# The causal mask of the scores as sixteen 32-row products instead of four 128-row ones

## The chip, the cores and the metric

The kernel runs on one core of one Trainium2 chip. The metric is the device time of one execution in microseconds, the median of several runs.

## The reference

A decoder layer over 32 sequences (batches) of 256 tokens with 512 features. It has three parts, each followed by an addition to its input and a layer norm:

1. causal self-attention with 16 heads of 32 features and rotary positions,
2. an mLSTM cross part with 4 heads over a context,
3. attention over 4 heads of 64 features, which a router picks from 16 for each sequence.

The change lies in the first part. Cut to what matters there:

```python
qkv = x @ Wqkv
q, k, v = jnp.split(qkv, 3, axis=-1)            # 16 heads of 32
q, k = _apply_rope(q, k)
dist = idx[None, :] - idx[:, None]              # key minus query
allowed = (dist <= 0) & (dist >= -(w - 1))      # w = 256 = the sequence: causal only
scores = jnp.einsum('bhqd,bhkd->bhqk', q, k) / jnp.sqrt(jnp.float32(d))
scores = jnp.where(allowed[None, None], scores, -jnp.inf)
weights = jax.nn.softmax(scores, axis=-1)
out = jnp.einsum('bhqk,bhkd->bhqd', weights, v)
```

## The kernel before

Three stages, `a` (self-attention), `b` (mLSTM) and `c` (routed attention), work at the same time on three successive batches. Every stage is a generator on each engine; `in_turns` walks one step of the pipeline, and the strings in `ORDER` say, engine by engine, which stage's generator comes next. So every engine's program is a fixed sequence written out by hand, the same in each of the 34 steps (30 of them have all three stages). What binds engines to each other is semaphores: `Port.wait_ge` puts a wait ahead of an instruction.

All products of TensorE (PE) go through the helper `mm` (L581), all transposes through `tr` (L589), so the profile tells them apart by their tiles. Projections are made of three products each in fp32r halves (`mm3`).

The 16 heads go in four groups of four, `u` = 0 to 3. `scores(u)` makes the scores of the four heads of a group: it waits for the rotated q and k (`roped`) and for the exponentials that free the score banks (`exped`), then issues for the first 128 queries four products of 32 rows of the array (head j sits in rows 32j to 32j+31 and writes bank `ps_s[:, j]`), then four for the last 128 queries over all 256 keys. After that come four products over the whole array that add the causal mask: for each head `eye_bf` (a 128x128 identity in bf16) times `mask_bf` (-1e30 above the diagonal), into the two diagonal 128x128 blocks of its bank. The last of them raises `scored`, for which VectorE (DVE) waits in `maxes` (L1219); ScalarE (ACT) then makes the exponentials (`exps`, L931).

The four groups of a batch stand at four places of a step. This text calls them by what TensorE's program has next behind the mask:

- **place A** (u = 0): the products `ps_g<-log_f,const` of stage b,
- **place B** (u = 1): the projection `ps_g<-x_t_hi,w_sel_hi` of stage c,
- **place C** (u = 2): the transposes `ps_g<-const,p_a` of this stage,
- **place D** (u = 3): the products `ps_g<-pt_all,v_f` of stage c.

Other names: `p_t` the transposed exponentials (copied out of PSUM by ACT L982 and DVE L1248), `k_f` stage c's keys (DVE L1441), `x_t_lo` the low half of a transposed operand (DVE L1472 for stage c's output), `v_a` the values of stage a (ACT L946).

Of the kernel before, what the change touches and what calls it, by code (L numbers as in the profile page):

```python
# [5 lines left out]
BF16 = mybir.dt.bfloat16  # L6
# [6 lines left out]
P = 128  # L13
NB, T, D = 32, 256, 512
TT, KT = T // P, D // P
HA, DA = 16, D // 16
# [3 lines left out]
DX = D // HX  # L20
# [4 lines left out]
Q_SCALE = float(np.float32(1.0 / np.sqrt(DA)))  # L25
LN_EPS, MLSTM_EPS, RMS_EPS = 1e-5, 1e-6, 1e-6
MASKED = -1e30
LOWEST = -3e38


# [75 lines left out]
    return np.concatenate([a.astype(np.float32) for a in parts.values()], axis=1), where  # L106


def build(nc, x, ctx, wqkv, wout, igk, igb, fgk, fgb, rms, wq, bq, wk, bk, wv, bv, wr, br, wo, bo, out):

    def sb(name, shape, dt=F32):
        return nc.alloc_sbuf_tensor(name, shape, dt).ap()
# [9 lines left out]
    const = sb("const", [P, table.shape[1]])  # L122
    c = {n: const[:, a:b] for n, (a, b) in where.items()}
    eye, upto = c["eye"], c["upto"]
    eye_bf = sb("eye_bf", [P, P], BF16)
    mask_bf = sb("mask_bf", [P, P], BF16)

    wqkv_s = halves("wqkv", [P, KT, 3 * D])
    wout_s = halves("wout", [P, KT, D])
# [4 lines left out]
    rms_w = sb("rms_w", [P, DX])  # L134
    bias_col = sb("bias_col", [P, 3, HF])
    wr_s = sb("wr_s", [P, KT, HF])
    br_s = sb("br_s", [1, HF])
    wo_s = halves("wo", [P, KF * DF // P, D])
    bo_s = sb("bo_s", [P, D])
# [13 lines left out]
    p_t = sb("p_t", [P, 4, CAUSAL])  # L153
# [54 lines left out]
    ps_s = nc.alloc_psum_tensor("ps_s", [P, 4, D], F32).ap()  # L208
# [3 lines left out]
    def count(name, per=1):  # L212
        return Count(nc, name, per)
# [3 lines left out]
    stage_hi, stage_split, tables_ready, half_ready = count("stage_hi"), count("stage_split"), count("tables_ready"), count("half_ready")  # L217
# [276 lines left out]
    def in_turns(s, engine, stages):  # L494
# [4 lines left out]
        for n, g in live.items():  # L499
# [5 lines left out]
    col = lambda w: w.rearrange("(k p) n -> p k n", p=P)  # L505
    row = lambda b, n: b.unsqueeze(0).to_broadcast([P, n])
# [6 lines left out]
    columns = [(wgate[:, :, j * HX:(j + 1) * HX], col(g[i * D:(i + 1) * D, :])) for i, wgate in enumerate((wgate_q, wgate_k, wgate_v)) for j, g in enumerate((igk, fgk))]  # L513
    columns += [(bias_col[half * DF:(half + 1) * DF, j, :], b.rearrange("(h d) -> d h", d=DF)) for j, b in enumerate((bq, bk, bv)) for half in range(2)]
    singles = [(const, nc.inline_tensor(table, name="tables").ap()), (gate_bias[:, 0:HX], row(igb, HX)), (gate_bias[:, HX:], row(fgb, HX)),
               (p_t[:, 0, 0:P], nc.inline_tensor(np.triu(np.full((P, P), MASKED, np.float32), 1), name="mask").ap()), (rms_w, row(rms, DX)), (wr_s, col(wr)), (br_s, br.unsqueeze(0)), (bo_s, row(bo, D))]
    SETUP = 16 * (len(columns) + len(singles))
    PIECES, Q_PIECES = len(pieces), 2

# [57 lines left out]
    def tensor(engine):  # L577
        pe = Port(engine)

        def mm(o, l, r, first, last):  # L580
            return nc.tensor.matmul(o, l, r, start=first, stop=last)  # L581
# [6 lines left out]
        def tr(o, i, ident):  # L588
            return nc.tensor.transpose(o, i, ident)  # L589
# [11 lines left out]
        def stage_a(b):  # L601
# [34 lines left out]
            def scores(u):  # L636
                pe.wait_ge(*roped(b, u + 1))
                if b or u:
                    pe.wait_ge(*(exped(b, 2 * u) if u else exped(b - 1)))
                for t in range(TT):  # L640
                    for j in range(4):
                        rows = slice(DA * j, DA * j + DA)
                        o = ps_s[:, j, t * P:t * P + P * (t + 1)]
                        done = mm(o, qk[rows, 2 * u, t * P:(t + 1) * P], qk[rows, 2 * u + 1, 0:P * (t + 1)], t == 0, False)
                for j in range(4):
                    o = ps_s[:, j, :].rearrange("p (a n) -> p a n", a=2)[:, :, 0:P]
                    done = mm(o, eye_bf, mask_bf.unsqueeze(1).to_broadcast([P, 2, P]), False, True)
                done.then_inc(scored.sem)

            yield from rotary(0)  # L650
            yield from values(0)
            scores(0)
            for _ in range(5):
                yield
            yield from values(1)
            yield from rotary(1)
            for u in range(QUADS):
                if u + 1 < QUADS:
                    scores(u + 1)
                for _ in range(3):  # L660
                    yield
                for p in (2 * u, 2 * u + 1):
                    for j in range(2):
                        o = bank[("turn", 2 * p + j), b]
                        pe.wait_ge(*exped(b, p + 1))
                        pe.wait_ge(*freed[("turn", 2 * p + j), b])
                        for n in range(3):
                            done = tr(o[:, n * P:(n + 1) * P], p_a[p % 2][:, j, n * P:(n + 1) * P], eye)
# [15 lines left out]
                o = bank[("att", u), b]  # L684
# [7 lines left out]
                for k in range(TT):  # L692
                    for j in range(4):
                        h = 4 * u + j
# [3 lines left out]
                        done = mm(o[strip, cols], v_a[:, k, h * DA:(h + 1) * DA], w, k == 0, k == TT - 1)  # L698
# [220 lines left out]
        pe.wait_ge(setup_loaded.sem, SETUP)  # L919
        pe.wait_ge(half_ready.sem, 5)  # L920
        pe.wait_ge(stage_split.sem, PIECES)
        pe.wait_ge(tables_ready.sem, 5)
        for s in range(NB + 2):
            in_turns(s, "tensor", {"a": stage_a, "b": stage_b, "c": stage_c})

# [1 line left out]
    def scalar(engine):  # L927
        act = Port(engine)
# [238 lines left out]
            else:  # L1167
                nc.scalar.copy(dst[0], stages[n % len(stages)]).then_inc(stage_hi.sem)
        act.wait_ge(setup_loaded.sem, SETUP)
        act.wait_ge(tables_ready.sem, 5)  # L1170
        act.wait_ge(half_ready.sem, 5)
        act.wait_ge(stage_split.sem, PIECES)
        for s in range(NB + 2):
# [3 lines left out]
    def vector(engine):  # L1177
        dve = Port(engine)
        v = nc.vector
# [112 lines left out]
        def stage_b(b):  # L1292
# [27 lines left out]
            dve.wait_ge(*empty[("a_row",), b])  # L1320
            v.tensor_tensor_scan(m_row, a_row, a_row, LOWEST, ALU.max, ALU.max).then_inc(m_scanned.sem)
            dve.wait_ge(*m_scanned(b))
# [201 lines left out]
            else:  # L1524
                v.tensor_tensor(dst[1], stages[n % len(stages)], dst[0].bitcast(F32), ALU.subtract).then_inc(stage_split.sem)
        dve.wait_ge(setup_loaded.sem, SETUP)
        v.tensor_copy(eye_bf, eye).then_inc(tables_ready.sem)
        v.tensor_copy(mask_bf, p_t[:, 0, 0:P]).then_inc(tables_ready.sem)
        v.tensor_copy(minus_pick, c["minus_pick"][0:LO_AT + HX]).then_inc(tables_ready.sem)
        v.tensor_tensor(wgate_k[:, :, 0:2 * HX], wgate_k[:, :, 0:2 * HX], wgate_v, ALU.add).then_inc(tables_ready.sem)  # L1530
        v.tensor_scalar(rms_w, rms_w, 1.0, None, ALU.add).then_inc(tables_ready.sem)
        dve.wait_ge(tables_ready.sem, 5)
        dve.wait_ge(stage_split.sem, PIECES)
        for s in range(NB + 2):
            in_turns(s, "vector", {"a": stage_a, "b": stage_b, "c": stage_c})
# [2 lines left out]
    def gpsimd(engine):  # L1538
        pool = Port(engine)
# [128 lines left out]
            g.memset(w[:, :, 2 * HX:], 0.0).then_inc(half_ready.sem)  # L1668
        g.tensor_scalar(m_parts, const[0:LO_AT + HX, 0:T], 0.0, None, ALU.mult).then_inc(half_ready.sem)
        pool.wait_ge(half_ready.sem, 5)  # L1670
        pool.wait_ge(tables_ready.sem, 5)
        for s in range(NB + 2):
            in_turns(s, "gpsimd", {"a": stage_a, "b": stage_b, "c": stage_c})

    with nc.Block() as block:
        block.tensor(tensor)
        block.scalar(scalar)
        block.vector(vector)
        block.gpsimd(gpsimd)
        block.sync(sync)  # L1680
# [22 lines left out]
```

## Time and profile before

| | |
|---|---|
| median of 3 runs | 2596.67 us (2593.72 to 2596.82) |
| the profiled execution's own time | 2597.26 us |
| its span (first to last instruction) | 2595.5 us |
| TensorE busy | 2319.3 us, 89% |
| VectorE busy | 1915.3 us, 74% |
| ScalarE busy | 1425.7 us, 55% |
| GpSimd busy | 702.2 us, 27% |
| granted TensorE clock | 0.98 of full |

The time is the device's; the span is what the trace covers, and lies 1.8 us below it. Busy shares are unions over the whole span; they say which engine could be the bound, not which one is at a given place. A matmul's duration in the trace contains a fixed latency, and matmuls overlap: what TensorE's time is made of is the distance from start to start.

### The profile page before, as it was taken

The page shows a single profiled execution, that of the slowest core. Times are in us where ns is not written, and L with a number is a line of the kernel's source. Part 1 is how long each engine was busy: PE and PEld are TensorE (multiplying, and loading weights), DVE is VectorE, ACT ScalarE, POOL GpSimd, SP SyncE. Part 2 cuts the span into 40 slices and gives each one's busy share as a digit, 9 for nine tenths or more (in the row PEclk, how much of TensorE's full clock was granted, in tenths as well). Part 3 has the DMA queues.
Part 4 walks back from the last instruction along what each step waited for, and adds up shares of the span by engine and source line. Part 5 has one row for each costly group of instructions (what it writes and reads, how often), then busy time and mean ns, then how long its engine had stood idle before and what let it go on. Part 6 is the DMA issues. An engine that isn't in the chain of part 4 may idle for free.

```text
span 2595.5 us, 52697 instructions
## 1 busy us (share of the span) xinstructions
PE 2319.3 (89%) x19200; PEld 1861.6 (72%) x19200; DVE 1915.3 (74%) x4590; ACT 1425.7 (55%) x4586; POOL 702.2 (27%) x1065
## 2 busy tenths in 40 slices
PE   3879999999999999999999999999999999999964
PEld 3657777777777777777777777777777777777753
DVE  3568777777777777877777777777787877777753
ACT  3445655565655556565556565555656555656532
POOL 0123232222233222223222223322222332222321
PEclk9999999999999999999999999999999999999976
DMA  4010111111111111011111111111101111111111
GB/s 111 17 33 26 42 42 50 50 42 31 44 34 50 50 50 42 26 42 42 50 50 42 33 42 34 50 50 50 42 26 42 42 50 50 43 34 32 34 33 41
DMA packets 267461, 109.70 MB, mean 42 GB/s; under 512 B 215234, under 2 KB 248258, under 8 KB 267202
## 3 DMA queue, kind: packets, MB, share of 16 engines
q1 hardware_dynamic: 258498, 89.54, 14.0%
q10 hardware_dynamic: 8704, 16.78, 1.7%
q8 instruction: 153, 2.51, 0.4%
q14 instruction: 106, 0.87, 0.1%
HBM read 89.51 MB, written 16.78 MB: 41 GB/s over the span
## 4 chain that ended last, share of the span: by engine, by line
PE 50%; DVE 29%; issue 9%; ACT 7%; POOL 3%; SPq 1%; DMA 1%; POOLq 0%; DVEq 0%; ACTq 0%
PE ps_g L581 37%; PE ps_g L589 8%; PE ps_s L581 5%; ACT p_a L931 4%; DVE neg_max L1219 3%; DVE decay L1339 2%; DVE qk L1212 2%; DVE ctx_t L1370 2%; DVE x_tok L1275 2%; POOL qk_rot L1557 2%; DVE ctx_t L1368 2%; DVE ln_stat_b L1182 1%; DVE ln_stat_a L1182 1%; DVE f_max L1450 1%; DVE r_dist L1407 1%
## 5 line engine op out<-in xcount | busy, mean ns | idle before, releaser
L931 ACT ACTIVATE p_a<-ps_s,neg_max 128x128 f32<-128x128 f32 (+1 forms) x1024 | 414.6, 438 | 64.0 <-DVE neg_max L1219 64.0
L581 PE MATMUL ps_g<-x_t_hi,wqkv_hi 128*128 128x256 f32 x1024 | 305.5, 298 | 22.9 <-DVE p_t L1248 21.5
L581 PE MATMUL ps_g<-x_t_lo,wqkv_hi 128*128 128x256 f32 x1024 | 287.3, 281 | 0.0
L581 PE MATMUL ps_g<-x_t_hi,wqkv_lo 128*128 128x256 f32 x1024 | 287.1, 280 | 0.0
L1219 DVE TENSOR_REDUCE neg_max<-ps_s 128x2 f32<-128x256 f32 (+1 forms) x512 | 258.7, 546 | 7.9 <-PE ps_s L581 7.9
L1644 POOL TENSOR_SCALAR p_all<-p_all,f_rec,g_bc 128x256 f32<-128x256 f32 x256 | 152.3, 607 | 367.5 <-DVE f_rec L1458 367.5
L1557 POOL TENSOR_TENSOR qk_rot<-qk_rot,const 128x512 f32<-128x512 f32 x128 | 164.4, 1284 | 298.3 <-DVE qk_rot L1205 298.3
L982 ACT COPY p_t<-ps_g 128x384 f32<-128x384 f32 x256 | 122.0, 478 | 199.8 <-PE ps_g L589 195.5
L931 ACT ACTIVATION_READ_ACCUMULATOR p_a<-ps_s,neg_max 128x1 f32 x1024 | 230.3, 225 | 0.0
L581 PEld LDWEIGHTS ps_g<-x_t_hi,wqkv_hi 128*128 128x128 f32 x1024 | 195.7, 191 | 40.0 <-DVE p_t L1248 27.6
L589 PE MATMUL ps_g<-const,p_a 128*128 128x128 f32 x1536 | 216.4, 278 | 5.5 <-DVE att_s L1265 2.3
L589 PEld LDWEIGHTS ps_g<-const,p_a 128*128 128x128 f32 x1536 | 172.6, 142 | 41.3 <-ACT p_t L982 12.4
L581 PEld LDWEIGHTS ps_g<-x_t_lo,wqkv_hi 128*128 128x128 f32 x1024 | 196.1, 192 | 0.0
L581 PEld LDWEIGHTS ps_g<-x_t_hi,wqkv_lo 128*128 128x128 f32 x1024 | 195.2, 191 | 0.0
L931 ACT ACTIVATE p_all<-ps_g,f_bias,g_bc 128x256 f32<-128x256 f32 x256 | 141.4, 559 | 55.1 <-DVE f_bias L1453 53.2
L581 PE MATMUL ps_g<-x_t_hi,w_sel_hi 128*128 128x256 f32 x512 | 147.1, 287 | 7.2 <-DVE w_sel_lo L1431 7.2
L1265 DVE TENSOR_TENSOR att_s<-ps_g,r_bc 128x256 f32<-128x256 f32 x128 | 54.3, 424 | 131.2 <-ACT r_bc L1004 128.7
L581 PE MATMUL ps_s<-qk 32*128 32x128 f32 (+1 forms) x2048 | 121.9, 352 | 25.7 <-ACT p_a L931 22.3
L581 PE MATMUL ps_g<-x_t_lo,w_sel_hi 128*128 128x256 f32 x512 | 144.6, 282 | 0.0
L581 PE MATMUL ps_g<-x_t_hi,w_sel_lo 128*128 128x256 f32 x512 | 144.2, 282 | 0.0
L1248 DVE COPY p_t<-ps_g 128x384 f32<-128x384 f32 x256 | 136.0, 541 | 3.6 <-PE ps_g L589 0.6
L1212 DVE TENSOR_TENSOR qk<-qk,qk_rot 128x512 f32<-128x512 f32 x128 | 124.1, 970 | 17.9 <-POOL qk_rot L1557 17.9
(203 smaller groups left out, 6299.5 us busy)
## 6 DMA issues: line engine op xcount, KB each, us to landing
x_tok<-in_x SPq DMA_DIRECT2D x32, 512.0 KB, 3.7
ctx<-in_ctx SPq DMA_DIRECT2D x64, 256.0 KB, 3.4
p_all<-in_L_ffn_Wq SPq DMA_DIRECT2D x128, 128.0 KB, 2.7
pt_all<-in_L_ffn_Wk SPq DMA_DIRECT2D x128, 128.0 KB, 3.0
y_out<-in_L_ffn_Wv SPq DMA_DIRECT2D x128, 128.0 KB, 3.2
out<-y_out ACTq DMA_DIRECT2D x32, 512.0 KB, 2.8
x<-in_L_attn_Wqkv SPq DMA_DIRECT2D x2, 512.0 KB, 7.8
p_all<-in_L_attn_Wqkv SPq DMA_DIRECT2D x1, 512.0 KB, 4.3
```

The costliest lines, as they stand in the source:

```text
L581: return nc.tensor.matmul(o, l, r, start=first, stop=last)
L589: return nc.tensor.transpose(o, i, ident)
L931: return nc.scalar.activation(o, i, f, **kw)
L982: nc.scalar.copy(p_t[:, 2 * p % 4, :], bank[("turn", 2 * p), b][:, 0:CAUSAL]).then_inc(act_emptied.sem)
L1182: v.bn_stats(ln[which][0][:, t, :], y[:, t, :]).then_inc(ln_stats[which].sem)
L1212: v.tensor_tensor(qk[:, 2 * u:2 * u + 2, :], qk[:, 2 * u:2 * u + 2, :], qk_rot, ALU.add).then_inc(roped.sem)
L1219: m = v.tensor_reduce(neg_max[i][:, :, t], ps_s[:, 2 * i:2 * i + 2, t * P:t * P + P * (t + 1)], AX.X, ALU.max, negate=True)
L1248: v.tensor_copy(p_t[:, (2 * p + 1) % 4, :], bank[("turn", 2 * p + 1), b][:, 0:CAUSAL]).then_inc(dve_emptied.sem)
L1265: v.tensor_tensor(att_s, bank[("att", u), b][:, 0:T], r_bc, ALU.mult).then_inc(dve_emptied.sem)
L1275: v.tensor_tensor(y_a[b % 2][:, t, :], bank[("out", t), b], x_tok[b % 2][:, t, :], ALU.add).then_inc(dve_emptied.sem)
L1557: g.tensor_tensor(qk_rot, qk_rot, c["sin"].unsqueeze(1).to_broadcast([P, 2, T]), ALU.mult).then_inc(sin_scaled.sem)
L1644: n = g.tensor_scalar(p_f[k % 2][:, t, :], p_f[k % 2][:, t, :], f_rec[:, k, t:t + 1], g_bc[:, k:k + 1], ALU.mult, ALU.mult)
```

## The change

The identity `eye_bf` and the 128x128 mask go. A new table `causal_mask()` has for each strip of 32 rows the same 256 columns: 224 columns `pick` and 32 columns `past`. Row i of `past` (i < 31) holds -1e30 above the diagonal of a 32x32 block, row 31 holds -1e30 everywhere. A window of 128 columns of `pick` (another one for each block of 32 keys) sends a query to the row of `past` that it needs: to row 31 if it lies wholly before the block, to row i if it is the block's query i, to none if it is past it. So one product of 32 rows masks 32 keys for 128 queries of both diagonal blocks; four key blocks times four heads make 16 products in place of four. Head j's products use rows 32j to 32j+31, as its score products do.

```diff
+def causal_mask():
+    past = np.triu(np.full((DA, DA), MASKED, np.float32), 1)
+    past[DA - 1] = MASKED
+    pick = np.zeros((DA, 2 * P - DA), np.float32)
+    pick[DA - 1, 0:P - DA] = 1.0
+    pick[0:DA - 1, P - DA:P - 1] = np.eye(DA - 1)
+    return np.tile(np.concatenate([pick, past], axis=1), (P // DA, 1))
...
-    eye_bf = sb("eye_bf", [P, P], BF16)
-    mask_bf = sb("mask_bf", [P, P], BF16)
+    mask_bf = sb("mask_bf", [P, MASK_COLS], BF16)
+    mask_past = mask_bf[:, MASK_COLS - DA:]
...
-                for j in range(4):
-                    o = ps_s[:, j, :].rearrange("p (a n) -> p a n", a=2)[:, :, 0:P]
-                    done = mm(o, eye_bf, mask_bf.unsqueeze(1).to_broadcast([P, 2, P]), False, True)
+                for block in range(P // DA):
+                    for j in range(4):
+                        rows = slice(DA * j, DA * j + DA)
+                        o = ps_s[:, j, :].rearrange("p (a n) -> p a n", a=2)[:, :, DA * block:DA * (block + 1)]
+                        done = mm(o, mask_bf[rows, P - DA * (block + 1):2 * P - DA * (block + 1)], mask_past[rows].unsqueeze(1).to_broadcast([DA, 2, DA]), False, block == P // DA - 1)
                 done.then_inc(scored.sem)
...
-        v.tensor_copy(eye_bf, eye).then_inc(tables_ready.sem)
-        v.tensor_copy(mask_bf, p_t[:, 0, 0:P]).then_inc(tables_ready.sem)
+        v.tensor_copy(mask_bf, p_t.rearrange("p h n -> p (h n)")[:, 0:MASK_COLS]).then_inc(tables_ready.sem)
```

The load of the mask at the start brings 256 columns instead of 128, and the waits on `tables_ready` count to 4 instead of 5.

Nothing else moves. This is TensorE's program at place D, in the order of the built program, before:

```order
L581 MATMUL ps_g<-p_t,v_a 32x128 x4
L581 MATMUL ps_s<-qk 128x128 [waits exped,qk_roped]
L581 MATMUL ps_s<-qk 128x128 x3
L581 MATMUL ps_s<-qk 128x256 x4
L581 MATMUL ps_s<-mask_bf,eye_bf 128x2x128 x4
L581 MATMUL ps_g<-pt_all,v_f 64x256 [waits bank_emptied_by_act,bank_emptied_by_dve]
```

and with the change (the helper `mm` has moved to L593):

```order
L593 MATMUL ps_g<-p_t,v_a 32x128 x4
L593 MATMUL ps_s<-qk 128x128 [waits exped,qk_roped]
L593 MATMUL ps_s<-qk 128x128 x3
L593 MATMUL ps_s<-qk 128x256 x4
L593 MATMUL ps_s<-mask_bf 128x2x32 x16
L593 MATMUL ps_g<-pt_all,v_f 64x256 [waits bank_emptied_by_act,bank_emptied_by_dve]
```

Only the row of the mask differs, 16 products of 64 columns for 4 of 256; the neighbours and their waits are the same, here and at the other three places.

## Rows read from the trace of the kernel before

**Rows 1.** The page: TensorE's share, and the chain that ended last, by engine

```profile
PE 2319.3 (89%) x19200; PEld 1861.6 (72%) x19200; DVE 1915.3 (74%) x4590; ACT 1425.7 (55%) x4586; POOL 702.2 (27%) x1065
...
PE 50%; DVE 29%; issue 9%; ACT 7%; POOL 3%; SPq 1%; DMA 1%; POOLq 0%; DVEq 0%; ACTq 0%
```

**Rows 2.** Chain in order of time, one step (start us, us, what)

```profile
1218.93 1.41 PE ps_s L581 x20
...
1225.51 1.48 PE ps_s L581 x20
...
1272.67 1.41 PE ps_s L581 x20
```

**Rows 3.** Waits of TensorE: us in total, times, longest us

```profile
PE ps_g L581 <- ACT v_a L946: 18.6, 30, 0.6
```

**Rows 4.** Timeline of TensorE at place D (start us, us, what, [idle before])

```profile
1225.51 0.94 PE L581 MATMUL ps_s<-qk 32*128 32x128 f32 x16 [0.70 <-ACT p_a L931]
1226.38 0.61 PE L581 MATMUL ps_s<-mask_bf,eye_bf 128*128 128x256 bf16 x4
1226.92 1.08 PE L581 MATMUL ps_g<-pt_all,v_f 128*64 128x256 f32 x8
```

**Rows 5.** Tile ps_s: durations in ns, least/median/most

```profile
L581 PE MATMUL ps_s<-qk x2048: 270/374/631, 46.3 to 2452.4; 32*128 32x128 f32 x94, 32*128 32x256 f32 x93
...
L581 PE MATMUL ps_s<-mask_bf,eye_bf x512: 272/273/421, 47.2 to 2453.0; 128*128 128x256 bf16 x171
```

**Rows 6.** Timeline of TensorE, narrow windows: first score strips; 15 tiny products

```profile
1225.51 0.39 PE L581 MATMUL ps_s<-qk 32*128 32x128 f32 x4 [0.70 <-ACT p_a L931]
...
1250.95 0.53 PE L581 MATMUL ps_g<-wr_s,x_sum 128*1 128x16 f32 x15
```

**Rows 7.** Weight loads grouped by shape: busy us, mean ns | idle before

```profile
L589 PEld LDWEIGHTS ps_g<-const,p_a 128*128 128x128 f32 x1536 | 172.6, 142 | 41.3 <-ACT p_t L982 12.4 <-issue 11.9 <-DVE x_t_lo L1472 6.1
...
L581 PEld LDWEIGHTS ps_g<-x_t_hi,w_sel_hi 128*128 128x128 f32 x512 | 97.7, 191 | 7.6 <-DVE w_sel_lo L1431 7.3
...
L581 PEld LDWEIGHTS ps_s<-qk 32*128 32x128 f32 x2048 | 70.5, 187 | 60.9 <-issue 53.1 <-DVE qk L1212 4.1
...
L581 PEld LDWEIGHTS ps_s<-mask_bf,eye_bf 128*128 128x128 bf16 x512 | 39.9, 98 | 46.7 <-issue 43.4
...
L581 PEld LDWEIGHTS ps_g<-wr_s,x_sum 128*1 128x1 f32 x512 | 14.0, 81 | 13.0 <-DVE x_sum L1393 9.2
```

**Rows 8.** VectorE behind place D and behind place B: timeline

```profile
1228.56 0.48 DVE L1472 SCALAR_TENSOR_TENSOR x_t_lo<-ps_g,b_v,x_t_hi 128x256 fp32r<-128x256 f32 x1 [0.51 <-ACT x_t_hi L931]
...
1279.78 0.48 DVE L1441 TENSOR_SCALAR k_f<-ps_g,b_sel 128x256 f32<-128x256 f32 x1 [0.37 <-PE ps_g L581]
```

**Rows 9.** Timeline of TensorE at place B

```profile
1272.60 0.94 PE L581 MATMUL ps_s<-qk 32*128 32x128 f32 x16
...
1273.84 0.36 PE L581 MATMUL ps_g<-x_t_hi,w_sel_hi 128*128 128x256 f32 x1
1274.04 0.28 PE L581 MATMUL ps_g<-x_t_lo,w_sel_hi 128*128 128x256 f32 x1
```

**Rows 10.** Timeline: a projection right after products in another tiling of the array

```profile
1238.18 0.50 PE L581 MATMUL ps_g<-wout_hi,x_t_hi 128*128 128x512 f32 x1
...
1238.52 0.40 PE L581 MATMUL ps_g<-wout_lo,x_t_hi 128*128 128x512 f32 x1
1238.75 0.39 PE L581 MATMUL ps_g<-wout_hi,x_t_lo 128*128 128x512 f32 x1
```

**Rows 11.** Timeline of TensorE at place C

```profile
1219.73 0.61 PE L581 MATMUL ps_s<-mask_bf,eye_bf 128*128 128x256 bf16 x4
1220.17 1.15 PE L589 MATMUL ps_g<-const,p_a 128*128 128x128 f32 x9
```

**Rows 12.** ScalarE behind place C: timeline, and the group on the page

```profile
1220.83 1.00 ACT L982 COPY p_t<-ps_g 128x384 f32<-128x384 f32 x2
...
L982 ACT COPY p_t<-ps_g 128x384 f32<-128x384 f32 x256 | 122.0, 478 | 199.8 <-PE ps_g L589 195.5
```

More of the change, by code:

```diff
@@ L27 @@
 MASKED = -1e30
+MASK_COLS = 2 * P
 LOWEST = -3e38
@@ L515, in build @@
     singles = [(const, nc.inline_tensor(table, name="tables").ap()), (gate_bias[:, 0:HX], row(igb, HX)), (gate_bias[:, HX:], row(fgb, HX)),
-               (p_t[:, 0, 0:P], nc.inline_tensor(np.triu(np.full((P, P), MASKED, np.float32), 1), name="mask").ap()), (rms_w, row(rms, DX)), (wr_s, col(wr)), (br_s, br.unsqueeze(0)), (bo_s, row(bo, D))]
+               (p_t.rearrange("p h n -> p (h n)")[:, 0:MASK_COLS], nc.inline_tensor(causal_mask(), name="mask").ap()), (rms_w, row(rms, DX)), (wr_s, col(wr)), (br_s, br.unsqueeze(0)), (bo_s, row(bo, D))]
     SETUP = 16 * (len(columns) + len(singles))
@@ L921, in tensor @@
         pe.wait_ge(stage_split.sem, PIECES)
-        pe.wait_ge(tables_ready.sem, 5)
+        pe.wait_ge(tables_ready.sem, 4)
         for s in range(NB + 2):
@@ L1169, in scalar @@
         act.wait_ge(setup_loaded.sem, SETUP)
-        act.wait_ge(tables_ready.sem, 5)
+        act.wait_ge(tables_ready.sem, 4)
         act.wait_ge(half_ready.sem, 5)
@@ L1531, in vector @@
         v.tensor_scalar(rms_w, rms_w, 1.0, None, ALU.add).then_inc(tables_ready.sem)
-        dve.wait_ge(tables_ready.sem, 5)
+        dve.wait_ge(tables_ready.sem, 4)
         dve.wait_ge(stage_split.sem, PIECES)
@@ L1670, in gpsimd @@
         pool.wait_ge(half_ready.sem, 5)
-        pool.wait_ge(tables_ready.sem, 5)
+        pool.wait_ge(tables_ready.sem, 4)
         for s in range(NB + 2):
```

## The prediction

> **What bounds the kernel now.** I read the page first: TensorE is busy 89% of the span, and half of the chain that ended last is its work, the rest mostly VectorE [rows 1]. So TensorE's time counts at some places of a step and not at others, and the question for each of the four mask places is whether it lies on that chain. The chain in order of time answers: in the step from 1202 to 1279 us it runs through three groups of 20 records (16 of scores, 4 of mask), those of places C, D and B in that order [rows 2]; the fourth, at place A, it leaves out. The list of waits says why: behind A's mask TensorE waits 0.6 us for ScalarE's copy of `v_a`, 30 times [rows 3]. That count is also the number of steps to which this reasoning applies; the first two and last two steps I leave at zero.
>
> **How the array's time is read.** A row's length contains the latency of its last record. At place D the scores start at 1225.51 and last 0.94, the last record's 0.374 included [rows 4, 5], so the last strips start at 1226.08, the first of that round 0.02 earlier (four strips start within (0.39 - 0.37) us, about 7 ns apart [rows 6]), at 1226.06. A round of four strips with 256 float32 columns streams for about 0.22: the eight `pt_all` records last 1.08, which is three distances plus 0.38 latency and some 0.05 for the first load [rows 4]. So the array was free for more strips at 1226.28, but the mask starts at 1226.38: about 0.10 goes to the change from strips to the whole array. The four mask products last 0.61 less 0.273 for the last [rows 4, 5], so they start 0.11 apart and the last at 1226.72; `pt_all` (again another tiling) starts at 1226.92, which is 0.11 of streaming and 0.09 of change. The mask so holds TensorE from 1226.28 to 1226.92 at D, of which only 0.44 is products.
>
> **The cost of the new products.** 256 columns take 0.11, so 64 take 0.027. The new ones use the same strips as the scores: no change of tiling ahead of them, and four run side by side. What one round of four costs, call it R, the trace does not show: no 32-row bf16 load stands in it. Bounds: starts 7 ns apart make at least 4 x 7 = 28 ns, and 15 products of 16 columns on one tile start (0.53 - 0.176) / 14 = 25 ns apart [rows 6], so R is at least 0.028. The load of 128 columns decides the rest. A load of one column lasts 81 ns; I take that as latency. The bf16 load of the old mask lasts 98, so its columns take 17 ns; a transpose's float32 load 142, so 61; a projection's float32 load 191, so 110 [rows 7]. A load in a strip of 32 rows is no dearer than one of 128: 187 for the scores' float32 ones, and four of them run at once [rows 6, 7]. The new load is nearest to the old mask's (same type, same 128 columns), 17 ns, hidden below the 28. I take R = 0.028; 0.06 and 0.11 are the dearer ends.
>
> The Trainium skill, "TensorE: Matmul & The Clock Gate", section "Weight-path perf modes", says that the fast load is on for a full 128-column weight that isn't FP32, which the new ones are; it says that it uses four of the array's buses, and nothing on four strips at once. By the rule R stays at the floor; if four fast loads took turns it would be some 4 x 17 ns, no more than the 0.06 above.
>
> **The sum, place by place.** New: first mask round where the array is free; three more rounds, 3R; the last strip 0.02 after the first; 0.03 streaming; then the change of tiling, 0.09, which used to stand ahead of the mask and now stands behind it. Together 0.14 + 3R.
> - *D:* next work at 1226.28 + 0.14 + 0.084 = 1226.50 instead of 1226.92: **0.42** saved. There the change of tiling behind the mask was paid before as well, so the one ahead of it is gone altogether. Does it pass on? VectorE's `x_t_lo` behind it waited 0.51 [rows 8], so it can come 0.42 earlier; then a long stretch of TensorE alone follows. Yes.
> - *B:* scores at 1272.60 [rows 9], free at 1272.60 + 0.94 - 0.374 - 0.02 + 0.22 = 1273.37; next work at 1273.59. But now the change of tiling also exposes the first float32 load: after such a change a projection's second product came 0.34 behind the first, where 0.23 is usual [rows 10], 0.11 more. So the second product of the projection starts at 1273.59 + 0.11 + 0.11 = 1273.81, before at 1274.04 [rows 9]: **0.23** saved. VectorE's `k_f` behind this stretch waited 0.37 for TensorE [rows 8], so it follows by 0.23.
> - *C:* before, the nine transposes started 0.11 behind the last mask product (1219.73 + 0.61 - 0.27 = 1220.07; 1220.17 to the row's digits [rows 11]). With the array free 0.10 ahead of the mask, at 1219.63 as at D, they now start at 1219.63 + 0.14 + 0.084 = 1219.85 and lose 0.05 on the first exposed load (half the projection's, as its load is half as long), so the group ends 0.27 earlier. ScalarE's two copies behind it last 1.00 where two alone take 0.96 [rows 12]: it waited for TensorE 0.04 and was busy with older work before that. So **0.04** passes on; then ScalarE's exponentials are the path up to D.
> - *A:* nothing; TensorE waits for `v_a` behind it [rows 3], and no wait in that stretch of the chain is for `scored`.
> - *Setup:* one cast less and one twice as wide on VectorE, once; I leave it at nothing.
>
> 30 x (0.42 + 0.23 + 0.04) = 20.7 us. Against the profiled execution's own time: 2597.26 - 20.7 = 2576.6; the median of the runs shown is 0.6 below that execution, so 2576.0. I say **2576**.
>
> With R = 0.06: D 0.32, B 0.13, C 0.04, in all 14.7 us, 2582. With R = 0.11: D 0.17, B -0.02, C 0.02, in all 5.1 us, 2591.6. Low end: if C's 0.27 passed on whole, 27.6 us, 2569.
>
> **Rivals.**
> 1. *The strips' bf16 loads are dearer* (R = 0.06 to 0.11). For it: no such load is in the trace. Against: the strips' float32 loads cost no more than whole ones. 2582 to 2591.
> 2. *The gain is swallowed*: VectorE and ScalarE are close behind. The cover that I allow at D is 0.51 against 0.42, at B 0.37 against 0.23 [rows 8]. If D's were lost to some queue that I overlooked, 30 x 0.27 remain: 2589; if both, no change.
> 3. *Slower: the 16 products go one at a time.* If loads in strips took turns at the 61 ns of a transpose's load, a round is 0.24: at D the next work comes at 1226.28 + 0.14 + 0.72 = 1227.14, 0.22 late; at B 0.41 late, at C 0.36 late, all on the chain: 30 x 0.99 = 30 us, 2626. It decides from about R = 0.13, 33 ns a product: there the gains at D (0.50 - 3R) and B (0.31 - 3R) are eaten by each other and by C. Against it: the first four score strips started 7 ns apart right after a real wait for `p_a` [rows 6], when nothing can have been queued past the wait, so neither the loads nor the issue of products takes turns there.
>
> The skill's page "TensorE: Matmul & The Clock Gate", section "Wait — 56ns, not 53.3ns?", has a rule that would bring that third rival about: with hardware decode off the sequencer needs about 62 ns for every matmul. By that rule an estimate of 16 x 62 ns = 1.0 us a group follows, and a time near rival 3's. The four strips 7 ns apart and the 25 ns of the tiny products speak against it here.
>
> **Chances.** Forecast (R near 0.03, gains pass) 0.48, its own range 2571 to 2580; rival 1 0.30, a third of it near R = 0.11, which is on the border of what can be told; rival 2 0.12, half of it over the border; rival 3 0.06; more than forecast 0.04. What a measurement of this kernel can tell from no change is about 0.2%, 5.2 us, so "faster" begins below 2591.5. Faster: 0.48 + 0.26 + 0.06 + 0.04 = 0.84, say 0.83; slower 0.06; the rest same. Range: from 2570 to 2592, which takes in all of rival 1 and leaves out rival 3, the unchanged half of rival 2 and little below.
>
> **What the profile after would show.** TensorE with 1536 more products (128 groups x 12), 20736 records. At D a mask row of 16 records, some 0.3 long (3R + 0.02 + one latency of about 0.2), starting 0.22 instead of 0.32 behind the last scores' round, and `pt_all` some 0.99 behind the first score instead of 1.41. If R is wrong, it shows in that row's length: 0.40 for R = 0.06, 0.55 for 0.11, 0.9 if they take turns. At C ScalarE's idle time is unchanged and TensorE's wait before the next transposes grows by some 0.2; at A its wait for `v_a` grows by 0.2 to 0.3. Every full step should be shorter by about 0.7. I would be wrong if the load in strips is slow, if the tiling changes cost more behind short products than behind long ones, or if VectorE's or ScalarE's slack at D or B is less than these two waits say.

## The result and the profile after

| | before | with the change |
|---|---|---|
| median | 2594.98 us (2590.37 to 2596.82, 6 runs) | 2576.95 us (2573.69 to 2578.44, 6 runs) |
| span of the profiled execution | 2595.5 us | 2576.1 us |
| granted TensorE clock | 0.98 | 0.974 |

The ratio is 0.9928, 95% interval 0.9917 to 0.9939: 0.72% faster, which is 18.7 us; the two medians are 18.0 us apart. The forecast was 2576, between 2570 and 2592.

The page of the changed kernel, its lines on the span, the engines and the chain:

```profile
span 2576.1 us, 55768 instructions
...
PE 2293.4 (89%) x20736; PEld 1866.1 (72%) x20736; DVE 1915.4 (74%) x4589; ACT 1424.4 (55%) x4586; POOL 702.4 (27%) x1065
...
PE 47%; DVE 28%; ACT 10%; issue 10%; POOL 3%; SPq 1%; DMA 1%; POOLq 0%; DVEq 0%; ACTq 0%
```

TensorE has 1536 more products and 26 us less busy time; VectorE and GpSimd are as before. The chain has less of TensorE (47% for 50%) and more of ScalarE (10% for 7%): where TensorE got out of the way, ScalarE shows.

One full step of it, in TensorE's timeline, with the four places in the order A, B, C, D and the start of the next A (other rows are left out at the dots):

```profile
1323.63 0.94 PE L593 MATMUL ps_s<-qk 32*128 32x128 f32 x16
1324.39 0.29 PE L593 MATMUL ps_s<-mask_bf 32*128 32x64 bf16 x16
1325.73 0.80 PE L593 MATMUL ps_g<-log_f,const 128*128 128x4 f32 x6 [1.05 <-ACT v_a L960]
...
1340.20 0.94 PE L593 MATMUL ps_s<-qk 32*128 32x128 f32 x16
1340.96 0.29 PE L593 MATMUL ps_s<-mask_bf 32*128 32x64 bf16 x16
1341.19 0.39 PE L593 MATMUL ps_g<-x_t_hi,w_sel_hi 128*128 128x256 f32 x1
1341.41 0.28 PE L593 MATMUL ps_g<-x_t_lo,w_sel_hi 128*128 128x256 f32 x1
...
1362.95 0.94 PE L593 MATMUL ps_s<-qk 32*128 32x128 f32 x16
1363.71 0.29 PE L593 MATMUL ps_s<-mask_bf 32*128 32x64 bf16 x16
1363.93 1.20 PE L601 MATMUL ps_g<-const,p_a 128*128 128x128 f32 x9
...
1369.44 0.94 PE L593 MATMUL ps_s<-qk 32*128 32x128 f32 x16 [0.70 <-ACT p_a L945]
1370.17 0.33 PE L593 MATMUL ps_s<-mask_bf 32*128 32x64 bf16 x16
1370.42 1.08 PE L593 MATMUL ps_g<-pt_all,v_f 128*64 128x256 f32 x8
...
1399.49 0.72 PE L593 MATMUL ps_s<-qk 32*128 32x128 f32 x12
```

At D the next work starts 0.98 behind the first score; before it was 1226.92 - 1225.51 = 1.41 [rows 4]. At B the projection's second product starts 1.21 behind the first score, before 1.44 [rows 9]. The mask row at C is 0.29 long, one latency of 0.188 in it, so sixteen products start within 0.10 us (at D the first strip comes a little ahead of the others and the row is 0.33).

The ways between the places, from the first score of one to the first score of the next, show what of it passes on. Before, the first scores of A, C and the A before B stood here:

```profile
1195.91 0.94 PE L581 MATMUL ps_s<-qk 32*128 32x128 f32 x16
...
1218.86 0.94 PE L581 MATMUL ps_s<-qk 32*128 32x128 f32 x16
...
1256.03 0.94 PE L581 MATMUL ps_s<-qk 32*128 32x128 f32 x16
```

(1195.91 is B's, 1218.86 C's, 1256.03 the next A's; D's is in [rows 4], the next B's in [rows 9].)

| from the scores of | before | after | less |
|---|---|---|---|
| A to B | 1272.60 - 1256.03 = 16.57 | 1340.20 - 1323.63 = 16.57 | 0 |
| B to C | 1218.86 - 1195.91 = 22.95 | 1362.95 - 1340.20 = 22.75 | 0.20 |
| C to D | 1225.51 - 1218.86 = 6.65 | 1369.44 - 1362.95 = 6.49 | 0.16 |
| D to A | 1256.03 - 1225.51 = 30.52 | 1399.49 - 1369.44 = 30.05 | 0.47 |

The medians over the steps are 16.58, 22.94, 6.65, 30.47 before and 16.58, 22.75, 6.50, 30.04 after: 0.19, 0.15 and 0.43 less, 0.77 a step. Over the 29 steps from one A to the A 29 steps on that would be 22.3 us. But the trace has:

```profile
180.54 0.94 PE L593 MATMUL ps_s<-qk 32*128 32x128 f32 x16
...
2387.63 0.94 PE L593 MATMUL ps_s<-qk 32*128 32x128 f32 x16
```

2207.09 us in the changed kernel, and before, from 182.82 to 2405.68, 2222.86: only 15.8 less. Most of the rest is in seven steps whose way from A to B is 17.4 or so instead of 16.57. There TensorE's clock is at half. The last 0.7 are two single ways, one of 16.92 from A to B and one of 30.40 from D to A. The trace of every variant below has such a pair and the one before has none; where they come from was not traced. Four stretches that begin 3 us behind A, in four steps in a row:

```profile
core 0: us, PE busy (x) PEld busy (x) DVE busy (x) ACT busy (x) POOL busy (x), PEclk, DMA share, GB/s
487.70:491.10 3.40, 3.40 (x11) 2.44 (x11) 2.58 (x9) 2.17 (x11) 0.37 (x2) 0.50 0.40 88
564.40:567.80 3.40, 3.29 (x15) 2.06 (x14) 3.30 (x10) 2.17 (x11) 0.37 (x2) 1.00 0.55 124
640.30:643.70 3.40, 3.27 (x15) 2.03 (x14) 3.30 (x10) 2.19 (x11) 0.37 (x2) 1.00 0.53 120
716.40:719.80 3.40, 3.40 (x10) 2.43 (x11) 2.60 (x9) 2.21 (x11) 0.37 (x2) 0.50 0.55 125
```

The column to read is PEclk: 0.50 is the lower of TensorE's two levels, 1.2 GHz. In the first stretch the projection's products of 512 columns run 0.43 apart, where they run 0.23 apart at the full 2.4 GHz [rows 10]:

```profile
488.05 0.63 PE L593 MATMUL ps_g<-wqkv_lo,x_t_hi 128*128 128x512 f32 x1
488.48 0.63 PE L593 MATMUL ps_g<-wqkv_hi,x_t_lo 128*128 128x512 f32 x1
488.91 0.63 PE L593 MATMUL ps_g<-wqkv_hi,x_t_hi 128*128 128x512 f32 x1
```

Six of the seven stretches begin three steps apart, from 487.7 to 1631.2 us, and none comes between there and the last full step. The trace before has no such stretch between its third step and the last full one. What precedes them is place A, where the change saved nothing and only lengthened a wait: TensorE is idle for 1.05 us until ScalarE's `v_a` is there, for 0.6 before [rows 3].

### The profile page after: what moved, and what is told of

It is laid out like the page before. It is cut to its first block, busy times and chain, and to the rows that moved or that the text cites. A ratio compares the mean times of both kernels' runs of the same rounds, so it can differ in the third digit from the quotient of the medians.

```text
span 2576.1 us, 55768 instructions
## 1 busy us (share of the span) xinstructions
PE 2293.4 (89%) x20736; PEld 1866.1 (72%) x20736; DVE 1915.4 (74%) x4589; ACT 1424.4 (55%) x4586; POOL 702.4 (27%) x1065
## 4 chain that ended last, share of the span: by engine, by line
PE 47%; DVE 28%; ACT 10%; issue 10%; POOL 3%; SPq 1%; DMA 1%; POOLq 0%; DVEq 0%; ACTq 0%
PE ps_g L593 38%; PE ps_g L601 7%; ACT p_a L945 4%; DVE neg_max L1233 3%; PE ps_s L593 3%; DVE qk L1226 2%; DVE decay L1353 2%; DVE ctx_t L1384 2%; DVE x_tok L1289 2%; POOL qk_rot L1570 2%; DVE ctx_t L1382 2%; DVE ln_stat_b L1196 1%; DVE ln_stat_a L1196 1%; DVE f_max L1464 1%; ACT p_all L945 1%
## 5 line engine op out<-in xcount | busy, mean ns | idle before, releaser
L593 PE MATMUL ps_g<-x_t_hi,wqkv_hi 128*128 128x256 f32 x1024 | 304.5, 297 | 19.0 <-DVE p_t L1262 17.6
L593 PE MATMUL ps_g<-x_t_lo,wqkv_hi 128*128 128x256 f32 x1024 | 286.1, 279 | 0.0
L593 PE MATMUL ps_g<-x_t_hi,wqkv_lo 128*128 128x256 f32 x1024 | 285.8, 279 | 0.0
L601 PE MATMUL ps_g<-const,p_a 128*128 128x128 f32 x1536 | 223.4, 284 | 4.2 <-ACT p_t L996 1.4
L593 PEld LDWEIGHTS ps_g<-x_t_hi,wqkv_hi 128*128 128x128 f32 x1024 | 194.8, 190 | 36.0 <-DVE p_t L1262 23.7
L593 PEld LDWEIGHTS ps_g<-x_t_lo,wqkv_hi 128*128 128x128 f32 x1024 | 195.4, 191 | 0.0
L593 PEld LDWEIGHTS ps_g<-x_t_hi,wqkv_lo 128*128 128x128 f32 x1024 | 194.4, 190 | 0.0
L593 PE MATMUL ps_g<-x_t_hi,w_sel_hi 128*128 128x256 f32 x512 | 147.9, 289 | 7.0 <-DVE w_sel_lo L1445 7.0
L593 PE MATMUL ps_s<-qk 32*128 32x128 f32 (+1 forms) x2048 | 122.6, 354 | 26.4 <-ACT p_a L945 22.9
L593 PE MATMUL ps_g<-x_t_lo,w_sel_hi 128*128 128x256 f32 x512 | 144.1, 281 | 0.0
L593 PE MATMUL ps_g<-x_t_hi,w_sel_lo 128*128 128x256 f32 x512 | 144.0, 281 | 0.0
```

## The experiments

All were timed beside the kernel before. A kernel that needs the mask over the whole array makes it from the new tables: the same 16 products with all 128 rows. The four copies of the table add up, so its mask value is -4e30; it is no less masked. The edit, here with strips at B, C and D alone:

```diff
+STRIP_PLACES = (1, 2, 3)
...
-                        rows = slice(DA * j, DA * j + DA)
+                        rows = slice(DA * j, DA * j + DA) if u in STRIP_PLACES else slice(0, P)
...
-                        done = mm(o, mask_bf[rows, P - DA * (block + 1):2 * P - DA * (block + 1)], mask_past[rows].unsqueeze(1).to_broadcast([DA, 2, DA]), False, block == P // DA - 1)
+                        done = mm(o, mask_bf[rows, P - DA * (block + 1):2 * P - DA * (block + 1)], mask_past[rows].unsqueeze(1).to_broadcast([rows.stop - rows.start, 2, DA]), False, block == P // DA - 1)
```

| kernel | median, us | ratio to before, 95% | A to B | B to C | C to D | D to A | idle at A | half-clock stretches |
|---|---|---|---|---|---|---|---|---|
| before | 2594.98 | | 16.58 | 22.94 | 6.65 | 30.47 | 0.62 | 0 |
| the change | 2576.95 | 0.9928 (0.9917 to 0.9939) | 16.58 | 22.75 | 6.50 | 30.04 | 1.05 | 7 |
| 16 whole-array products everywhere | 2600.51 | 1.0016 (1.0006 to 1.0025) | 16.58 | 23.03 | 6.72 | 30.51 | 0.59 | 0 |
| strips at D only | 2585.91 | 0.9960 (0.9946 to 0.9974) | 16.57 | 23.03 | 6.73 | 30.04 | 0.59 | 0 |
| strips at C only | 2593.17 | 0.9990 (0.9980 to 0.9999) | 16.58 | 23.03 | 6.51 | 30.49 | 0.59 | 0 |
| strips at B only | 2593.96 | 0.9993 (0.9984 to 1.0003) | 16.58 | 22.76 | 6.73 | 30.49 | 0.60 | 0 |
| strips at A only | 2603.01 | 1.0029 (1.0019 to 1.0038) | 16.58 | 23.04 | 6.72 | 30.50 | 1.05 | 2 |
| strips at B, C, D | 2573.47 | 0.9911 (0.9896 to 0.9926) | 16.58 | 22.77 | 6.49 | 30.05 | 0.59 | 0 |

Each ratio is to the runs of the kernel before on the same chip. The whole-array kernel and those with strips at D, at A and at B, C, D shared one chip (before: 2596.03), those with strips at C and at B another (before: 2595.43), so a comparison across the two goes by the ratios. The ways, in us, are medians over the full steps in each trace. Idle at A is TensorE's wait for `v_a` behind the mask. A half-clock stretch is one in which the granted clock is 0.50; those between the third step's A and the last full step's are counted.

**The same 16 products over the whole array, at all places.**

> The same 16 products of 64 columns, with the same tables, but each over all 128 rows of the array at all four places (the four copies of the table add up, so the mask value is four times as large). My theory: the gain comes from running four strips side by side and from dropping the change of tiling ahead of the mask, not from fewer columns. Then 16 products start one after another 25 to 28 ns apart, 0.40 to 0.45 us, against 0.44 for the four old ones, with the old changes of tiling: within 0.2% of before, about 2595 us. Rival: the gain comes from streaming a quarter of the columns; then this one is near 2577.

2600.51 us, 1.0016 of before: the rival is out by 24 us. TensorE at its place D, the score row, the mask row and what follows:

```profile
1305.65 0.94 PE L594 MATMUL ps_s<-qk 32*128 32x128 f32 x16 [0.70 <-ACT p_a L946]
1306.52 0.64 PE L594 MATMUL ps_s<-mask_bf 128*128 128x64 bf16 x16
1307.09 0.87 PE L594 MATMUL ps_g<-pt_all,v_f 128*64 128x256 f32 x6
```

The row less one latency of 0.19 is 0.45 for 15 distances, 30 ns a product, for a quarter of the columns of the old ones (which were 0.11 apart). So 16 short products take as long as the four long ones, and the mask starts 0.87 behind the scores and not 0.73 as in strips. The next work at D starts 1.44 behind the scores here and 0.98 in strips; of these 0.46, 0.14 is the earlier start of the mask and 0.31 its shorter row. At B and C the mask starts 0.76 behind the scores in strips, so the earlier start is 0.11 there. The kernel is a little slower than before, though within the 0.2% of the expectation: 0.09 more from B to C, 0.07 from C to D, 0.04 from D to A, 6 us in 30 steps by these medians, 4.7 us by the 29 full steps of the traces. This kernel, not the one before, is what the single places are compared with.

**Strips at D only.**

> Strips at place D alone. My theory: 30 x 0.43 us = 13 us faster than whole-array products at all places, about 2582 us, with TensorE's next work 0.43 earlier and no half clock in the steady steps. Rival: part of D's gain is swallowed by ScalarE or VectorE: less than 9 us.

2585.91, 14.6 below the whole-array kernel; D to A falls from 30.51 to 30.04 and nothing else moves. D passes its gain on whole.

**Strips at C only.**

> Strips at place C alone, whole-array products elsewhere. With strips everywhere the way from C's scores to D's is 6.50 us, with whole-array products everywhere 6.72, before 6.65. My prediction gave this place only 0.04 us. Theory now: ScalarE waited for TensorE's transposes behind C for 0.16 and not 0.04, since two copies with no wait between them take less than twice one; so the way from C to D is 6.50 here too, 30 x 0.22 = 6.6 us less than whole-array products everywhere, about 2594. Rival: C's 0.16 came with the earlier start that B gives its surroundings; then the way from C to D here stays at 6.6 or above, and the kernel saves under 3 us.

2593.17, 7.3 below by the medians and 6.7 by the ratios, and C to D is 6.51, as with strips everywhere: the 0.16 is C's own. ScalarE shows where it comes from. In the changed kernel, the two copies behind C and what follows them:

```profile
1364.92 0.85 ACT L996 COPY p_t<-ps_g 128x384 f32<-128x384 f32 x2
1365.64 0.42 ACT L1005 COPY r_wide<-p_rec 128x256 f32<-128x256 f32 x1
```

and with whole-array products:

```profile
1300.89 1.08 ACT L997 COPY p_t<-ps_g 128x384 f32<-128x384 f32 x2
1301.87 0.41 ACT L1006 COPY r_wide<-p_rec 128x256 f32<-128x256 f32 x1
```

Two copies that wait for nothing last 0.85, not twice 0.478, since the second starts about 0.1 before the first has ended; the next copy starts 0.72 behind the first. Before, that pair lasted 1.00 [rows 12]. So ScalarE waited for TensorE there for 0.15, not for the 0.04 that I had by subtracting two means.

**Strips at B only.**

> Strips at place B alone. Theory: the way from B's scores to C's falls from 23.03 (whole-array products) to 22.75 us, 30 x 0.28 = 8 us less than with whole-array products everywhere: about 2592. Rival: a part of it is C's; then the way from B to C stays above 22.85.

2593.96, 6.5 below by the medians and 6.0 by the ratios; B to C is 22.76. The single places add up: 0.47, 0.21 and 0.27 less than in the whole-array kernel for D, C and B alone, and 0.47, 0.22 and 0.28 with all of them.

**Strips at A only.**

> Strips at place A alone, 16 whole-array products at B, C and D. My theory: nothing saved at A, and the longer idle time there brings stretches of half clock in some of the steady steps: 2595 to 2602 us, slower than with whole-array products at all four places if the stretches come. Rival: the half clock needs the smaller total of work; then no stretches and the same time as with whole-array products at all places.

2603.01, a little above the 2595 to 2602 expected, against 2600.51 with whole-array products everywhere: 2.5 more, though the two intervals overlap. The four ways are the same in the median, the idle time at A is 1.05, and two stretches of half clock have come, with the work at B, C and D as long as it ever was. The first of them:

```profile
493.50:496.90 3.40, 3.40 (x11) 2.43 (x10) 2.97 (x9) 2.67 (x14) 0.19 (x1) 0.50 0.59 134
```

The third figure from the end, PEclk, is again 0.50. So the strips at A save nothing, and they alone can bring the stretches on.

**Strips at B, C and D, the whole array at A.**

> Strips at B, C and D, the 16 products over the whole array at place A alone. In the trace after the change seven of the steady steps have 0.83 us more between A and B, each with a stretch of 3.4 us at half the clock that begins some 3 us behind A. My theory: the longer idle time of TensorE behind A's mask (1.05 us, before 0.62) brings this on, and the strips save nothing at A. Then this kernel has no such stretch in the steady steps and is 7 x 0.83 = 6 us faster than the changed kernel: about 2571 us. Rival: the half clock comes from the smaller total of TensorE's work, or by chance; then the stretches stay and the time is within 2 us of 2577.

2573.47, 3.5 below the changed kernel by the medians and 4.4 by the ratios where 6 were expected, and no stretch left. Place A, and the clock behind it in four steps in a row:

```profile
1245.27 0.94 PE L594 MATMUL ps_s<-qk 32*128 32x128 f32 x16
1246.14 0.64 PE L594 MATMUL ps_s<-mask_bf 128*128 128x64 bf16 x16
1247.37 0.80 PE L594 MATMUL ps_g<-log_f,const 128*128 128x4 f32 x6 [0.59 <-ACT v_a L961]
```

```profile
489.00:492.40 3.40, 3.21 (x17) 2.02 (x16) 3.27 (x9) 2.55 (x13) 0.19 (x1) 1.00 0.57 128
565.00:568.40 3.40, 3.21 (x17) 2.06 (x15) 3.26 (x10) 2.65 (x14) 0.19 (x1) 1.00 0.67 151
641.00:644.40 3.40, 3.21 (x17) 1.99 (x15) 3.26 (x10) 2.76 (x15) 0.19 (x1) 1.00 0.74 168
717.00:720.40 3.40, 3.19 (x17) 2.03 (x15) 3.26 (x10) 2.58 (x13) 0.19 (x1) 1.00 0.69 157
```

The log_f products start 1247.37 - 1245.27 = 2.10 behind A's scores, in the changed kernel 1325.73 - 1323.63 = 2.10: the same. Less work at A means more waiting at A, and with the longer wait come the stretches. Since the two add up to the same 2.10, no run tells the longer wait from the lesser work ahead of it as the cause. The 29 full steps take 2201.8 us here, 5.3 less than in the changed kernel.

**The two loops of the mask exchanged: strip by strip.**

```diff
-                for block in range(P // DA):
-                    for j in range(4):
+                for j in range(4):
+                    for block in range(P // DA):
```

> The changed kernel with the two loops of the mask exchanged: four products in a row in one strip, then the next strip. The same 16 products, the same tables. Theory: products of one strip can't start closer than the 25 ns of the tiny products, but TensorE starts products in their order, so the 16 take about 16 x 25 = 0.40 us instead of 0.14: the next work 0.26 us later at D and B, 0.2 at C, about 2577 + 30 x 0.7 - some of the half-clock time = 2592 to 2598. Rival: TensorE takes up a strip's products ahead of another's that wait, so the order doesn't matter: 2577.

2578.20, ratio 0.9933 (0.9916 to 0.9949), the changed kernel's time. My theory fell. Its place D:

```profile
1287.40 0.94 PE L593 MATMUL ps_s<-qk 32*128 32x128 f32 x16 [0.70 <-ACT p_a L945]
1288.13 0.34 PE L593 MATMUL ps_s<-mask_bf 32*128 32x64 bf16 x16
1288.40 0.87 PE L593 MATMUL ps_g<-pt_all,v_f 128*64 128x256 f32 x6
```

The mask row is 0.34 long instead of 0.33, and the next work starts 1.00 behind the scores instead of 0.98. Whether TensorE starts another strip's product ahead of its turn, or products of one strip can start some 10 ns apart ((0.34 - 0.188) / 15), the trace can't tell, since its rows don't name the strip.

**Every mask product twice.**

```diff
-                for block in range(P // DA):
+                for turn in range(2 * P // DA):
+                    block = turn % (P // DA)
```

> The changed kernel with every mask product done twice (the mask value doubles): eight rounds of four strips instead of four. Theory: a round costs 0.028 us, so the next work comes 0.11 us later at B, C and D: 30 x 0.33 = 10 us, less what is regained where TensorE's idle time at A falls from 1.05 to 0.94: 2581 to 2587. Rival: rounds are dearer than the first four show (loads stop being hidden when they come in a row): 0.06 each, 0.24 a place, near 2598.

2578.42, ratio 0.9934 (0.9918 to 0.9951). Its place D:

```profile
1287.50 0.94 PE L593 MATMUL ps_s<-qk 32*128 32x128 f32 x16 [0.71 <-ACT p_a L946]
1288.23 0.45 PE L593 MATMUL ps_s<-mask_bf 32*128 32x64 bf16 x32
1288.61 0.65 PE L593 MATMUL ps_g<-pt_all,v_f 128*64 128x256 f32 x4
```

Four more rounds make the row 0.45 - 0.33 = 0.12 longer and the next work 0.13 later: 0.03 a round, with 16 loads more in a row. The ways grow by 0.09 (B to C), 0.03 and 0.12, which is 7 us in 30 steps; yet the time is only 1.5 above the changed kernel's, below the 2581 to 2587 that I expected, and the 29 full steps take 2208.1, 1.0 more. I had put too little on the clock: at A the idle time is 0.91, and no stretch of half clock is left.

**Twice at A alone, beside the changed kernel and the whole array at A.**

```diff
+                turns = 2 * P // DA if u == 0 else P // DA
+                for turn in range(turns):
+                    block = turn % (P // DA)
```

> The changed kernel with the mask products done twice at place A alone (the mask value doubles for those heads), where TensorE waits for ScalarE's copy of the values anyway. With them twice at all places TensorE's idle time at A was 0.91 us and no stretch of half clock came between the first and the last full step. Theory: the added products cost nothing at A, the idle time of about 0.91 keeps the clock up, and this kernel is as fast as the one with whole-array products at A: about 3 to 6 us below the changed kernel run beside it. Rival: it is the kind of products (128 rows) or the other places' added work that keeps the clock up; then the stretches stay and the time is that of the changed kernel.

> The changed kernel once more, on the chip of the two others of this call, to compare with directly: 2577 us, with several stretches of half clock in the full steps.

> Strips at B, C and D, whole-array products at A, once more beside the changed kernel: no stretch of half clock in the full steps, 3 to 6 us below the changed kernel.

| same chip | median, us | ratio to before, 95% | 29 full steps | idle at A | stretches |
|---|---|---|---|---|---|
| the change | 2577.78 | 0.9925 (0.9911 to 0.9938) | 2207.1 | 1.05 | 6 |
| twice at A | 2572.20 | 0.9914 (0.9900 to 0.9927) | 2202.1 | 0.91 | 0 |
| whole array at A | 2572.79 | 0.9909 (0.9895 to 0.9922) | 2201.8 | 0.59 | 0 |

```profile
1243.41 0.94 PE L593 MATMUL ps_s<-qk 32*128 32x128 f32 x16
1244.17 0.43 PE L593 MATMUL ps_s<-mask_bf 32*128 32x64 bf16 x32
1245.51 0.69 PE L593 MATMUL ps_g<-log_f,const 128*128 128x4 f32 x5 [0.91 <-ACT v_a L962]
```

Sixteen more products at A, which the computation doesn't need, take 5 us off the full steps, as much as the whole-array ones. So the kind of product is not what matters. By their medians the two versions are 5.6 and 5.0 us below the changed kernel, and about 22 below the one before: faster than both. The intervals of the ratios still overlap with the changed kernel's, since each run also varies by some microseconds in the first two steps, while the lengths of the full steps stand apart clearly: 2207.1, 2207.1 and 2207.3 in the three traces with six or seven stretches (the change twice, strip by strip), 2201.8, 2201.8 and 2202.1 in the three without any that have the same strips at B, C and D (the whole array at A in two traces, twice at A).

## Why the prediction was right, point by point

The mechanism at D, B and C held, and the total came close in part by luck. The forecast of 2576 stood on a median of 2596.67; over the six runs that median is 2594.98, so 1.7 less saving was needed to arrive there, and the medians differ by 18.0 where 20.7 were forecast. The terms inside missed by more and in both directions.

- **R = 0.028, the disputed cost: right.** The mask row at C is 0.29 with a latency of 0.188 in it, so (0.29 - 0.188 - 0.02) / 3 = 0.027; doubling the rounds gave 0.03. The strips' load, which no row before showed, is the cheap one. It lasts 94 ns in the mean, a little under the old mask's 98 [rows 7]. (Had four loads taken turns at 17 ns, the prediction's "4 x 17 ns, no more than the 0.06" would have been 0.068, a little more; nothing in the forecast hangs on it.)

```profile
L593 PEld LDWEIGHTS ps_s<-mask_bf 32*128 32x128 bf16 x2048 | 38.8, 94 | 14.1 <-issue 1.0
```

- **The change of tiling: right.** It stands behind the mask now: the next work at B starts 0.98 behind the scores, and the last mask product 0.76 + 0.29 - 0.188 = 0.86, which leaves 0.12, 0.03 of it streaming and 0.09 the change. D, where one is gone altogether, gained 0.43 where 0.42 was written; the gain at B, with the exposed load, was 0.23 at the projection's second product as written, of which 0.19 reached C. Where the other 0.04 went I did not trace.
- **"So 0.04 passes on" at C: mis-sized.** It was 0.15. The step took two mean durations from a row's length; back-to-back copies overlap. "ScalarE's idle time is unchanged" at C fell with it.
- **Place A, "nothing": right in the median, wrong in sum.** The prediction saw that TensorE's wait for `v_a` would grow by 0.2 to 0.3 (it grew by 0.43) and gave that no price. It cost the changed kernel seven stretches of half clock, about 17.41 - 16.58 = 0.83 each, some 6 us. That term was missing from the sum. C's 0.11 x 30 = 3.3 us too little made up for half of it, B's 0.04 x 30 = 1.2 too much did not, nor did the 0.7 of the two single long ways, and 3.6 us came off outside the 29 full steps (the spans differ by 19.4, those steps by 15.8), where the prediction had put nothing. 2.3 of them lie before the first of those steps, a stretch that ends anywhere from 175.5 to 183.6 us in the traces of this study, so I read nothing into them. 20.7 us were forecast, 18.7 measured by the ratio: the total is closer than its terms.
- **The ranges and rivals.** None of the three came as described; what the clock took back at A is a form of rival 2 that it did not name. Rival 3's serial products would have shown as a mask row of 0.9. The whole-array kernel is the nearest thing to it: 30 ns a product one after another, and no gain.
- **The cover behind D: right.** VectorE's `x_t_lo` there waited 0.51 and now waits 0.15:

```profile
1372.06 0.48 DVE L1486 SCALAR_TENSOR_TENSOR x_t_lo<-ps_g,b_v,x_t_hi 128x256 fp32r<-128x256 f32 x1 [0.15 <-ACT x_t_hi L945]
```

A second saving of this size at D would find it nearly used up; no run tried one.

## What to carry to other kernels

Look at what surrounds a small product on TensorE: a product in the same strips as its neighbours pays no change of tiling between them (the mask starts 0.11 to 0.14 us sooner behind the scores here) and shares its time with three others, while the same count over the whole array gained nothing here. Take each place where the product stands by itself, and ask what waits behind it. Where TensorE has to wait anyway, faster work only makes the pause longer, and with the longer pause clock can be lost in what follows: there the slow form, or more products than needed, did better here.

## What the runs showed of the hardware that I had not expected

- TensorE fell to its 1.2 GHz level within full steps when the pause at A was 1.02 to 1.05 us (7, 6, 6 and 2 stretches in four traces: the change twice, strip by strip, strips at A only) and never in the eight traces of variants with a pause of 0.59 to 0.91, nor before with 0.62. Why some kernels with the same pause have two stretches and others seven is open; the pause is not the only condition.
- The order of products among strips did not matter: four in a row in one strip cost 0.02 us more than four strips in turn.
- Whole-array bf16 products of 64 columns start 30 ns apart, those of 256 columns 110 ns.
- Two ScalarE copies of 0.478 us each in the mean, back to back, take 0.85 us.
